# Attention in a one-core language-model tower: the row of maxima spread over strips of 32 rows, for two blocks of keys at once

## What is computed

```python
D_MODEL, N_HEADS, D_HEAD = (192, 12, 64)          # batch 2, 2048 tokens
q = einsum('bsd,hde->bshe', x, W_Q) + b_Q         # k and v likewise
scores = einsum('bqhe,bkhe->bhqk', q, k) / sqrt(D_HEAD)
scores = where(causal, scores, -inf)
pattern = softmax(scores, axis=-1)
z = einsum('bhqk,bkhe->bqhe', pattern, v)
attn_out = einsum('bqhe,hed->bqd', z, W_O) + b_O
```

## Time and profile before

| | us |
|---|---|
| median of three runs | 2651.92 |
| lowest, highest | 2651.59, 2652.84 |
| profiled execution: its own time | 2648.46 |
| profiled execution: span of its instructions | 2646.7 |
| TensorE busy in the span | 2390.5 (90%) |

### The profile page before, as it was taken

One profiled execution on the slowest core, in us unless ns is written; L12 is line 12 of the kernel. 1 busy time (PEld: TensorE's weight loads), 2 busy tenths in 40 slices (PEclk: granted clock), 3 DMA queues, 4 the chain that ended last, 5 costly groups with the idle time before them and its releaser, 6 DMA issues. The chain is left out here.

```text
span 2646.7 us, 42215 instructions
## 1 busy us (share of the span) xinstructions
PE 2390.5 (90%) x16000; PEld 1225.3 (46%) x16000; DVE 1859.5 (70%) x3771; ACT 1231.6 (47%) x1728; POOL 1242.6 (47%) x858
## 2 busy tenths in 40 slices
PE   3565899999999999999999999996999999999998
PEld 1233555555555555555555556543333333333332
DVE  7864565656565656566565656687988989888987
ACT  3422233333333333333333333354777777777776
POOL 5000265756575757575756666663413323324120
PEclk9787899999999999999999999996999999999999
DMA  1002000000001000000000001131011000000000
GB/s 50 12 23 61 1 8 8 3 9 1 10 1 33 1 10 1 10 1 10 1 9 1 3 1 20 19 53 55 9 19 21 15 19 21 15 19 9 19 7 7
DMA packets 42940, 39.33 MB, mean 15 GB/s; under 512 B 26865, under 2 KB 35186, under 8 KB 41842
## 3 DMA queue, kind: packets, MB, share of 16 engines
q1 hardware_dynamic: 40608, 31.18, 5.3%
q0 software_dynamic: 1536, 3.15, 0.4%
q10 hardware_dynamic: 594, 2.31, 0.2%
HBM read 26.13 MB, written 10.49 MB: 14 GB/s over the span
## 5 line engine op out<-in xcount | busy, mean ns | idle before, releaser
L678 POOL TENSOR_TENSOR acc<-acc,pT 128x1024 f32<-128x1024 f32 (+3 forms) x412 | 836.0, 2029 | 239.7 <-ACT pT L1077 202.9
L1077 ACT ACTIVATE pT<-banks 128x1024 f32<-128x1024 f32 x480 | 406.7, 896 | 812.9 <-PE banks L751 747.2
L1806 DVE TENSOR_TENSOR hw<-hid,banks 128x512 f32<-128x512 f32 x1024 | 662.8, 680 | 84.0 <-PE banks L1489 69.6
L896 DVE TENSOR_REDUCE part<-banks 128x2 f32<-128x1024 f32 (+3 forms) x432 | 438.0, 1044 | 313.0 <-PE banks L727 311.3
L1648 ACT ACTIVATE hid<-banks 128x1024 f32<-128x1024 f32 x512 | 496.7, 1022 | 183.8 <-PE banks L1479 167.4
L767 PE MATMUL banks<-pT,v 128*64 128x512 f32 (+3 forms) x1920 | 405.5, 543 | 1.1 <-POOL pT L662 1.1
L1489 PE MATMUL banks<-wT,select 64*128 64x512 f16 x1024 | 341.6, 392 | 42.1 <-DVE hw L1806 22.5
L1479 PE MATMUL banks<-zst,w1c 50*128 50x512 f32 x1024 | 306.5, 541 | 10.7 <-ACT hid L1648 10.7
L1497 PE MATMUL banks<-hw,w 128*32 128x512 f32 x2048 | 278.3, 616 | 0.8 <-DVE hw L1806 0.8
L1489 PEld LDWEIGHTS banks<-wT,select 64*128 64x128 f16 x1024 | 93.7, 94 | 399.1 <-DVE hw L1806 340.2
L767 PEld LDWEIGHTS banks<-pT,v 128*64 128x64 f32 x1920 | 116.7, 136 | 203.1 <-issue 181.1
(11 more groups left out here) (228 smaller groups left out, 3161.4 us busy)
## 6 DMA issues: line engine op xcount, KB each, us to landing
zst<-z_scratch SPq DMA_DIRECT2D x48, 128.0 KB, 4.0
z_scratch<-zp SPq DMA_DIRECT2D x8, 512.0 KB, 2.8
out_h<-o SPq DMA_DIRECT2D x8, 384.0 KB, 2.6
xT_scratch<-xs_hi SPq DMA_DIRECT2D x4, 512.0 KB, 2.7
xt_hi<-xT_scratch SPq DMA_DIRECT2D x2, 1024.0 KB, 5.7
w<-in_L_ffn_W ACTq DMA_DIRECT2D x1, 2048.0 KB, 8.5
xt_hi<-in_L_ffn_W SPq DMA_DIRECT2D x12, 128.0 KB, 4.6
v<-in_L_ffn_W SPq DMA_DIRECT2D x12, 128.0 KB, 4.3
```

The lines of the kernel that those rows point to most:

```text
L678: pool.tensor_tensor(acc[:, G % 2, :, off:CH], acc[:, G % 2, :, off:CH], pT[:, slot, :, 0:w], ALU.add).then_inc(summed, 1)
L896: last = dve.tensor_reduce(to[:, :, c:c + 1], both[:, :, 0:whole], AX.X, ALU.max)
L1077: act.activation(pT[:, J % PSLOTS, :, 0:CH - off], both[:, :, 0:CH - off], ACT.Exp, scale=E ** -0.5)\
L1806: dve.tensor_tensor(hw[:, n % 2, q, :], hid[:, n % 2, q, :], ring_bank(("w", g, n, q)), ALU.mult).then_inc(mixed, 1)
```

## The change

`score_columns` now does both blocks of a step. It waits for the slots of both before its first product. The maxima of a head stand four times in `cpad`'s columns instead of twice: leading and rest part on rows 0 and 1 of each strip of 32 rows, two strips for each head. Four products of 32 rows each stand in a row, the two heads of block 2t and then the two heads of block 2t+1, on strips 0, 2, 1 and 3; then come the three terms of block 2t and the three of block 2t+1, as before with 64 rows. Nothing is added or removed in the number of products.

```diff
+    STRIP = 32
...
-            def score_columns(it, j):
-                banks = slot_free(place[("s2", it, j)])
+            def score_columns(it, t):
                 u = it % 2
-                Q, kt, off = key_block(j)
+                blocks = [(j, slot_free(place[("s2", it, j)])) for j in (2 * t, 2 * t + 1)]
+                Q, kt, _ = key_block(2 * t)
                 if kt == 0:
                     pe.wait_ge(rows_copied, it * NQC + Q + 1)
-                w = CH - off
-                t0 = Q * CH + off
-                for h in range(2):
-                    pe.matmul(banks[h][:, 0:w], ones[head(h), :], rows[head(h), u, Q, off:CH], start=True, stop=False)
+                for n, (j, banks) in enumerate(blocks):
+                    off = key_block(j)[2]
+                    for h in range(2):
+                        strip = slice((2 * h + n) * STRIP, (2 * h + n + 1) * STRIP)
+                        pe.matmul(banks[h][:, 0:CH - off], ones[strip, :], rows[strip, u, Q, off:CH],
+                                  start=True, stop=False)
                 terms = ((kh, qh), (kh, ql), (kl, qh))
-                for k, (a, b) in enumerate(terms):
-                    for h in range(2):
-                        last = pe.matmul(banks[h][:, 0:w], a[u][head(h), kt * P:(kt + 1) * P],
-                                         b[u][head(h), t0:t0 + w], start=False, stop=(k == 2))
-                last.then_inc(filled, 1)
+                for j, banks in blocks:
+                    _, kt, off = key_block(j)
+                    w, t0 = CH - off, Q * CH + off
+                    for k, (a, b) in enumerate(terms):
+                        for h in range(2):
+                            last = pe.matmul(banks[h][:, 0:w], a[u][head(h), kt * P:(kt + 1) * P],
+                                             b[u][head(h), t0:t0 + w], start=False, stop=(k == 2))
+                    last.then_inc(filled, 1)
...
-                leading, rest = (cpad[:, :, k:k + E + 1:E] for k in range(2))
+                leading, rest = (cpad[:, :, k:k + 3 * STRIP + 1:STRIP].rearrange("p t (h a) -> p t h a", a=2)
+                                 for k in range(2))
-                by_tile = negmax[:, :].rearrange("p (t h) -> p t h", h=2)
+                by_tile = negmax[:, :].rearrange("p (t h) -> p t h", h=2).unsqueeze(3).to_broadcast([P, TQ, 2, 2])
```

More of the change, by code:

```diff
@@ L829, in _ @@
                 for t in range(MACROS):
-                    score_columns(it, 2 * t)
-                    score_columns(it, 2 * t + 1)
+                    score_columns(it, t)
                     for item in PLAN[it][t]:
```

## The result

The changed kernel takes 2697.36 us (median of four runs, 2696.49 to 2698.89) against 2651.76 for the kernel before on the same occasions: a ratio of 1.0176, 95% interval 1.0159 to 1.0194. It is slower by about 46 us; the forecast was 2693.

What follows compares the result with a forecast made beforehand. PE was taken to bound the attention, 90% busy or more. Eleven units of 3.72 us (40.9) and the last unit, together 42.1 on 2651.92, gave 2693 us, 1.6% slower; range 2672 to 2715, for 8 in 10 2652 to 2728.

Steps and rivals of the forecast that it cites:

- Part 1: Ones products of each step: the second block's pair runs beside the first's, saving 0.23, 0.17 or 0.06 us by width.
- Part 2: Between 32-row ones products and 64-row terms: one added change of shape costs 0.20 us in each of 240 steps.
- The sign that I had named for it: In a wide step, from the first 32-row product to the first term: 0.54 us, against 0.34 by rival (a).
- rival (a): The change of shape is free and the four products run side by side: 2650 us, no change; chance 0.12.
- Part 3: ScalarE's exponentials for the two blocks: the later first block is paid whole, seven times 0.20, 1.40 us a unit.
- Part 4: Start of steps 3, 6, 13, 15: waiting for the second slot's release costs 0.92, 0.27, 0.32, 0.23; 1.74 us a unit.
- Narrow steps: Four steps a unit whose second block has 128 columns: each 0.14 us longer, 0.56 a unit.
- Part 5: VectorE's 48 pairs of cpad writes, 16 values instead of 8: nothing measurable; 7 us either way in the range.
- The last unit: The attention's last unit, with few side items: +0.35 us from its steps and +0.9 from the wait at step 12.
- The first unit: Start of the attention: counted like the others among the 11 units, at 3.72 us each.
- (b): Start of each step: the saved slot reaches every step's end, 44 us gained, 2608 us; chance 0.08 with what lies between.
- (c): Ones products: the four strips stream two and two, the first block full later still, 2732 us; chance 0.10.

Runs made afterwards that it cites:

- two-strips run: The changed kernel without the second block's ones products, their maxima left out of the output: 2693.05 us in one run.
- the four halves: The changed kernel with 64-row ones products, four in a row without a change of shape, and cpad written as before: 2696.86 us, ratio 1.0174.
- late-steps run: The changed kernel with steps 3, 6, 13 and 15 done block by block with 64 rows, as before: 2673.19 us, ratio 1.0087.
- the maximum of two inputs: The copy into cpad replaced by a two-input maximum: 2650.45 us (ratio 1.0004) in the kernel before, 2697.26 us (1.0177) in the changed kernel.
- strip-shape run: The kernel before with its ones products on one 32-row strip a head, order and waits unchanged: 2755.9 us, ratio 1.0399.
- wait-only run: The kernel before, waiting for both blocks' slots ahead of a step's first product, shapes and order unchanged: 2672.42 us, ratio 1.0085.

## Why the prediction was right

The forecast held in sign, size and mechanism. Of the 4.07 us that a unit costs, the late releases are 2.12 (1.74 forecast) and the rest 1.95 (1.98 forecast); outside the ten middle units the agreement is in part luck, as the last points show. The written 2693 is also 1 us under its own sum (2651.92 + 42.1 = 2694.0). Point by point:

- **Part 1** (the slot goes, four strips side by side): right, by the two-strips run.
- **Part 2** (a switch of 0.20 from strips to halves): right in size: 0.44 + 0.33 for 0.34 + 0.23, and 0.60 for three. The sign that I had named for it, 0.54 to the first term, did not come: it was 0.44, between mine and the 0.34 of rival (a), and the other 0.10 stood behind the first term. The drain that the TensorEngine Tiling page (Tiling Modes) of the Trainium skill names is seen in the 0.10; in this trace as much again is the load of weights that did not go ahead of the change.
- **Part 3** (ScalarE passes the later first block on): right, in the steps that I named, 0.19 to 0.22, and by the four halves independent of the switch. For step 12 it shows only in the late-steps run (+0.20): in the changed kernel the late release ahead of step 13 hides it, and with the moved wait alone step 12 grew as much (0.63).
- **Part 4** (late releases): right in place, wrong in two of four sizes. By the late-steps run they cost 0.98 ahead of step 3 (0.92 said), 0.12 ahead of step 6 (0.27 said; PE itself came 0.18 later there, which I had left out), 0.41 ahead of step 13 (0.61 less the 0.20 of step 12; 0.32 said) and 0.61 in steps 14 and 15. Step 15 was mis-sized. I kept 0.23 because VectorE's chain would swallow the rest, and with the moved wait alone the two steps did lose 0.22. In the changed kernel they lost 0.63. The rows of the sixth unit show why, first before, then after:

```profile
1023.54 0.49 PE L747 MATMUL banks<-zst,ones 64*128 64x512 f32 x2
1027.61 3.49 DVE L896 TENSOR_REDUCE part<-banks 128x2 f32<-128x1024 f32 x3
```
```profile
1044.40 0.50 PE L751 MATMUL banks<-zst,ones 32*128 32x512 f32 x4
1044.81 1.79 DVE L922 CAST cpad<-negmax 128x16 fp32r<-128x16 f32 x1
1048.69 3.49 DVE L903 TENSOR_REDUCE part<-banks 128x2 f32<-128x1024 f32 x3
1051.19 0.50 PE L751 MATMUL banks<-zst,ones 32*128 32x512 f32 x4 [0.54 <-DVE part L903]
```

  The copy into `cpad` ends 2.20 us after step 14's start where it was 2.00 (1025.54 in the earlier trace rows), again with GpSimd's addition (1046.55), and the reductions, the second of which frees the slot of step 15, start 4.29 after it for 4.07. So the release itself is 0.22 later, by the later first block, through ScalarE and GpSimd to the copy. I had reckoned with that path for steps 8 and 9 and not here. This is read from the rows; no run of the changed kernel takes the path away (the maximum of two inputs waited as long).
- **Narrow steps**: 0.08 to 0.10 instead of 0.14 in three, and 0.18 in step 5 (in the late-steps run), where a load of the first pass waits 0.16 us for ScalarE and did not before. The switch costs its 0.19 there too (the first term starts 0.31 after the ones products for 0.22, and keeps its pair 0.22 for 0.12), but the second block saves 0.11, the 0.06 of its ones pair and 0.05 of its first term, not 0.06.
- **Part 5** (nothing from the wider `cpad` writes): right. Its cause is not the copy alone.
- **The last unit** cost 3.1 us up to the start of its last step, where 1.2 was forecast. The wait at step 12 is there. Behind it 1.6 of the other 1.9 are TensorE's clock: it was granted 0.50 (1.2 GHz) from 1795.7 to 1799.1 us, and a pair of 512 columns took 0.43 us there for 0.23. First that stretch as in the earlier trace rows, then two rows of PE:

```profile
1795.70:1799.10 3.40, 3.40 (x20) 2.18 (x18) 0.32 (x1) 2.05 (x2) 1.04 (x1) 0.50 1.12 149
1794.71 0.50 PE L751 MATMUL banks<-zst,ones 32*128 32x512 f32 x4 [1.80 <-issue]
1796.13 0.63 PE L759 MATMUL banks<-qh,kh 64*128 64x512 f32 x2
```

  PE had been idle for 1.80 us ahead of the step. In the two-strips run it was idle for 1.82 at the same place, the clock stayed at 1.00, and step 12 took 1.58 less. So this is not a cost of every execution, and what decides it is not shown.
- **The first unit** was counted like the others, and the second unit starts only 1.6 us later. Steps 2 to 19 of it cost 4.0 as elsewhere, and its start is 2.0 later, but its first two steps are 4.35 shorter. In the trace before, the clock was halved (0.50) in part of them, told as in the earlier trace rows:

```profile
299.50:306.30 6.80, 6.80 (x26) 3.81 (x27) 0.00 (x0) 1.58 (x3) 4.63 (x6) 0.50 0.00 0
```

  In the changed kernel it was 1.00 there. My estimate of what that stretch cost the kernel before is half of its 6.8 us, 3.4. The forecast knew of neither stretch; they pull in opposite ways.
- **Behind the attention** the changed kernel took 2.7 us longer in this execution, and 2.2 in the two-strips run; I have no cause for it.

The sum for the profiled execution: ten units of 4.05, the last unit's 3.1, 2.7 behind it and 1.6 ahead of the second unit make 48, the difference of the spans (2694.7 - 2646.7). My 2690.6 for it was 5.9 low (2696.49): 3.3 in the ten units, 1.9 in the last and 2.7 behind it, less 2.1 in the first.

Rival (a) fell with the strip-shape run, (b) with it and with the wait-only run, (c) with the two strips.

## What to carry to other kernels

A saved product is worth what reaches the end of the step. Here the slot was saved in the block that nothing waited for, and it was paid by the block on which ScalarE's chain hangs. Count the changes of a product's shape, not only products: at 0.2 us a change, a trick with smaller tiles must save more than one slot of 512 columns between two changes. When two waits are put together, look up for each step when the later one is released; the trace before has those times. Then ask whether the change moves the release too, as it did here in step 14. And compare the granted clock of the same stretch in both traces before a difference at the edges is read as a cost.

## What the runs showed of the hardware that I had not expected

- Products of 32 and of 64 rows do not mix for free although both use whole strips: 0.10 us until the array takes the next shape and 0.10 for weights not loaded ahead; three switches a step cost 0.60 us, in both directions.
- With 32-row strips four products of 512 columns started within 0.011 us and cost together what two cost (131.05 and 131.03 us a unit).
- A tiny VectorE write from SBUF waited up to 1.57 us for GpSimd's addition, as a copy with one input and as a maximum of two, while a reduction of 40 values beside the same additions took 0.196 to 0.198 us in all 48 calls. Taking the wait from one instruction hands it to the next one that has the waiting form.
- After an idle 1.80 us in the last unit TensorE's granted clock fell from 1.00 to 0.50 for 3.4 us in one execution, and after 1.82 at the same place it did not in another.
